# Adding up the routed expert results in memory by the scatter itself, in two buffers used in turn

## The chip, the cores and the metric

The kernel runs on one core of one Trainium2 chip. The metric is the device time of one execution in microseconds, as the median of several runs.

## The reference, cut to what matters

The reference is one transformer layer on 8 sequences of 256 tokens with 256 features (2048 tokens): attention, then a feed-forward part with two shared experts and 16 routed experts, of which each token uses 4. The second part is

```
h = _layernorm(x) * (1 + cb) + sb
scores = sigmoid(h @ gate_w.T)                 # 16 experts in 4 groups, 2 groups kept, 4 experts chosen
w = scores of the 4 chosen / their sum         # cw[t, e]: w at the chosen experts, else 0
hh = silu(einsum('td,edh->teh', h, w1)) * einsum('td,edh->teh', h, w3)
y = einsum('teh,ehd,te->td', hh, w2, cw)       # the sum over each token's 4 routed experts
z = silu(h @ sw1) * (h @ sw3) @ sw2            # the shared experts
out = x + gb * (y + z)
```

The change concerns the sum over a token's four experts in `y`.

## The kernel before

The work is tiled by 128 tokens: 16 tiles (NT). `attention` works through the 8 sequences in a software pipeline. Its routing part runs on VectorE in `choose`, in six groups of tiles: it finds the four experts of each token, writes the weights into `hrow` behind the token's 256 features and, behind those, 16 numbers that say to which row of `y_d` the result of each expert goes: row 4 * token + k for the k-th choice. `send_rows` then scatters each token's row four times from POOL (GpSimd) into `rows_d`, where each expert has its own stretch of rows. At the end of the attention SP (the queue of SyncE) writes zeros over the head of each expert's stretch (L373) and stores the last tiles of x (L362).

`experts` has one unrolled stream of units that TensorE (PE), ScalarE (ACT) and VectorE (DVE) each go through in order: 8 shared tiles, 80 routed tiles (TILES) of 128 rows for one expert each, then the other 8 shared tiles, each shared tile with two units. A unit is: transpose x (L1389), six up matmuls (L1406 to L1408), the gate on ACT and DVE (L1202, L1263 or L1266, and the copy L1268), transpose (L1414, L1415), its split into a high and a low part (L1207, L1272), five down matmuls into `y_ps` (L1429 to L1433). SP loads each routed tile's rows into a ring of six buffers `xin` (L1158). A routed tile's result is copied by ACT to one of three buffers `yout` (L1218), and POOL scatters it to `y_d` by an indirect DMA (L1183), 128 rows of 1 KB. Rows of a tile that hold no token go to spare rows at the end of `y_d`. Only ACT waits on such a scatter, for the buffer: the scatter of tile t - 3 must have landed before tile t is copied.

After the last scatter SP loads, for each of the 16 token tiles in the order of `finals` (0, 8, 1, 9, ...), four rows of 1 KB for each token (`yt`, 512 KB), and the stored x (`x1t`). POOL adds two times two rows (L1187, 128x512) and then two (L1189, 128x256). `combine` on DVE adds the shared result (L1281 from `hrow`, L1285 from `y_ps`), multiplies by `gb` (L1288) and adds x (L1291); SP stores. The pair of tiles (t, t + 8) is combined in DVE's stream four steps behind the unit of tile t + 8, so DVE does it before what follows of the shared units, and the down matmuls of a shared tile wait until the pair two before has left `y_ps`. `gb` comes by eight broadcast loads that SP issues behind the last `xin` (L1161).

Of the kernel before, what the change touches and what calls it, by code (L numbers as in the profile page):

```python
# [53 lines left out]

ROW = HID + 2 * E

# [4 lines left out]
SLOT_ROWS = E * CAP  # L61
Y_ROWS = TOPK * NT * P + TILES * P

# [8 lines left out]
def constants():  # L72

    inv = (1.0 / np.float32(THETA) ** (np.arange(0, D, 2, dtype=np.float32) / np.float32(D))).astype(np.float32)
    freqs = np.arange(S, dtype=np.float32)[:, None] * inv[None, :]
    cos, sin = np.cos(freqs).astype(np.float32), np.sin(freqs).astype(np.float32)
    rope = np.stack([np.concatenate([cos, cos], 1), np.concatenate([-sin, sin], 1)], 1)
    rope = rope.reshape(QT, P, 2, D).transpose(1, 2, 0, 3)
    lower = (np.arange(G)[None, :] < np.arange(G)[:, None]).astype(np.float32)
    key, col = np.arange(P)[:, None], np.arange(SC)[None, :]  # L80
    key, query = np.where(col < K1, key + P, key), np.where(col < K1, col + P, col - K1)
    allowed = (key <= query) & (key > query - WINDOW)
    p = np.arange(P)
    wide = lambda x: np.ascontiguousarray(np.broadcast_to(np.asarray(x, np.float32).reshape(1, -1), (P, np.size(x))))
    fill = P * np.arange(E)
    fill[0] = -1
    return {
        "mask": np.where(allowed, 0.0, -1e5).astype(np.float32),
        "rope": np.ascontiguousarray(rope),
        "ident": np.eye(P, dtype=np.float32),  # L90
        "before": (p[:, None] < p[None, :]).astype(np.float32),
        "small": np.concatenate([
            wide(lower),
            wide(np.arange(E)),
            wide(CAP * np.arange(E) + P),
            wide(fill),
            (TOPK * (np.arange(NT)[None, :] * P + p[:, None])).astype(np.float32),
            (TOPK * NT * P + np.arange(TILES)[None, :] * P + p[:, None]).astype(np.float32),
            p[:, None].astype(np.float32),
            (p[:, None] - P).astype(np.float32),  # L100
            (P * p[:, None]).astype(np.float32),
        ], 1),
    }
# [3 lines left out]
for _name, _n in (("lower", G * G), ("iota", E), ("base", E), ("fill", E), ("tok", NT), ("spare", TILES), ("row", 1), ("behind", 1), ("rows", 1)):  # L107
# [12 lines left out]
ROUTE1 = ("sig biased gmax ggt geq geqm ggt rank gfar*2 maskg masked top*N idx*N idxf onehot picked pick cum*N "  # L120
          "wsel wsum*2 cw id2 id3 ids")
ROUTE2 = "place place_k slot_f slots"
# [11 lines left out]
def build(nc, a, out):  # L134

    with ExitStack() as whole:
# [8 lines left out]
        rows_d = nc.dram_tensor("rows_d", [SLOT_ROWS, ROW], F32, kind="Internal").ap()  # L145
        y_d = nc.dram_tensor("y_d", [Y_ROWS, HID], F32, kind="Internal").ap()

# [23 lines left out]
        })  # L171
        attention(nc, a, mod_rows, x1d, rows_d, hrow, gate_t, ident, w, r)
        sb("w_rest", [P, E - EARLY + SHARED, WE])
# [53 lines left out]

def attention(nc, a, mod_rows, x1d, rows_d, hrow, gate_t, ident, w, r):
    with ExitStack() as ctx:
# [3 lines left out]
        def sem(name):  # L233
# [73 lines left out]
            "c_in w_in wmod_in wo_in ct_tanh_done ct_silu_done cols_mm rows_mm cols_done rows_copied rows_neg_done "  # L307
            "rows_sign_done rows_sign2 rows_done rows_stored x1_stored zeros_set heads_zeroed consts_set pool_consts probs_set wqkvh_done wqkvl_done woh_done wol_done "
            "stats_done mv_done var_eps rstd_done xhat_done xhat_t ht_done hth_done htl_done qkv_mm qkv_done rcos_done rsin_done "
# [17 lines left out]
        def _(sp):  # L327
# [604 lines left out]
def scratch(alloc, n):  # L932

    return named({
        "sig": alloc("sig", [P, n, E], F32), "biased": alloc("biased", [P, n, E], F32), "gmax": alloc("gmax", [P, n, G], F32),
        "g_gt": alloc("g_gt", [P, n, G, G], F32), "g_eq": alloc("g_eq", [P, n, G, G], F32), "rank": alloc("rank", [P, n, G], F32),
        "gfar": alloc("gfar", [P, n, G], F32), "top": alloc("top", [P, n, 8], F32), "idx": alloc("idx", [P, n, 8], U32),
        "idxf": alloc("idxf", [P, n, TOPK], F32), "onehot": alloc("onehot", [P, n, TOPK, E], F32), "picked": alloc("picked", [P, n, E], F32),
        "pick": alloc("pick", [P, n, E], BF16), "wsel": alloc("wsel", [P, n, E], F32), "wsum": alloc("wsum", [P, n], F32),
        "id2": alloc("id2", [P, n, E], F32), "id3": alloc("id3", [P, n, E], F32), "place": alloc("place", [P, n, E], F32),  # L940
        "place_k": alloc("place_k", [P, n, TOPK, E], F32), "slot_f": alloc("slot_f", [P, n, TOPK], F32),
    })
# [7 lines left out]
def choose(dve, r, g, hrow, m):  # L950
# [59 lines left out]
    dve.tensor_tensor(gate_t, g.wsel[:, 0:n], g.wsum[:, 0:n].unsqueeze(2).to_broadcast([P, n, E]), ALU.mult).then_inc(r.worked, 1)  # L1010
    dve.scalar_tensor_tensor(out=g.id2[:, 0:n], in0=g.onehot[:, 0:n, 2], scalar=2.0, in1=g.onehot[:, 0:n, 1], op0=ALU.mult, op1=ALU.add).then_inc(r.worked, 1)
    dve.wait_ge(r.worked, at("id2"))
    dve.scalar_tensor_tensor(out=g.id3[:, 0:n], in0=g.onehot[:, 0:n, 3], scalar=3.0, in1=g.id2[:, 0:n], op0=ALU.mult, op1=ALU.add).then_inc(r.worked, 1)
    dve.wait_ge(r.worked, at("id3"))
    dve.tensor_tensor(hrow[:, here, HID + E:ROW].bitcast(I32), g.id3[:, 0:n], c("tok")[:, here].unsqueeze(2).to_broadcast([P, n, E]), ALU.add).then_inc(r.worked, 1)

# [33 lines left out]
def experts(nc, a, out, mod_rows, x1d, rows_d, y_d, hrow, gate_t, tab, w, r, ident):  # L1050


    with ExitStack() as ctx:
# [19 lines left out]
        def within(name, shape, dt):  # L1073
# [20 lines left out]

        yt = nc.alloc_sbuf_tensor_at("yt", [P, NT, TOPK * HID], F32, offset=address(nc, w.routed))
        x1t = nc.alloc_sbuf_tensor_at("x1t", [P, NT, HID], F32, offset=address(nc, w.routed) + 4 * NT * TOPK * HID)
        gb = w.raw[:].rearrange("p a n -> p (a n)")[:, 0:B * HID].rearrange("p (b h) -> p b h", b=B)
# [9 lines left out]
        s = named({n: sem("f_" + n) for n in (  # L1107
            "xt xh xl up silu hid dup ht hth htl down evac to summed stored added1 added2 gated spread").split()})
        x_in = [sem(f"f_x_in{j}") for j in range(XR)]
        y_sent = [sem(f"f_y_sent{j}") for j in range(YR)]  # L1110
        yt_in = [sem(f"f_yt_in{t}") for t in range(NT)]
# [33 lines left out]
        def _(sp):  # L1145
# [14 lines left out]
            for b in range(B):  # L1160
                sp.dma_start(gb[:, b], mod_rows[b:b + 1, 3].to_broadcast([P, HID])).then_inc(gb_in, 16)  # L1161
            for j in range(YR):
                sp.wait_ge(y_sent[j], 16 * len(range(j, TILES, YR)))
            for c, t in enumerate(finals):
                rows = y_d[t * P * TOPK:(t + 1) * P * TOPK].rearrange("(p k) h -> p (k h)", k=TOPK)
                sp.dma_start(yt[:, t], rows).then_inc(yt_in[t], 16)
                if t % 4 == 0:
                    sp.dma_start(x1t[:, t:t + 4], x1d[t:t + 4].rearrange("t p h -> p t h")).then_inc(x1_in[t // 4], 16)
# [5 lines left out]
        def _(pool):  # L1174
# [5 lines left out]
            for i in range(TILES):  # L1180
                pool.wait_ge(s.evac, FIRST + i + 1)
                pool.wait_ge(s.to, i + 1)
                pool.indirect_dma_start(y_d, bass.IndirectOffsetOnAxis(ap=to[:, i:i + 1], axis=0), yout[:, i % YR], None)\  # L1183
                    .then_inc(y_sent[i % YR], 16)
            for c, t in enumerate(finals):
                pool.wait_ge(yt_in[t], 16)
                pool.tensor_tensor(yt[:, t, 0:2 * HID], yt[:, t, 0:2 * HID], yt[:, t, 2 * HID:4 * HID], ALU.add).then_inc(s.added1, 1)  # L1187
                pool.wait_ge(s.added1, c + 1)
                pool.tensor_tensor(yt[:, t, 0:HID], yt[:, t, 0:HID], yt[:, t, HID:2 * HID], ALU.add).then_inc(s.added2, 1)  # L1189

        @block.scalar
        def _(act):
# [16 lines left out]
            def evacuate(j):  # L1209
# [5 lines left out]
                else:  # L1215
                    if t >= YR:
                        act.wait_ge(y_sent[t % YR], 16 * (t // YR))
                    act.activation(yout[:, t % YR], y_ps[:, j % 2, 0:HID], ACT.Copy).then_inc(s.evac, 1)  # L1218
# [22 lines left out]
        def _(dve):  # L1241
# [257 lines left out]
```

## Time and profile before

| | |
|---|---|
| median of 3 runs | 565.77 us (563.22 to 567.87) |
| profiled execution, its own time | 564.4 us |
| its span | 562.6 us |
| busy: PE, DVE, POOL, ACT | 416.2, 392.8, 296.8, 234.6 us |
| granted clock of TensorE, mean | 0.826 |

The span is what the profile covers; the device time has 1.8 us more. An engine's busy time says little by itself, since the stages have different limits: the rows below are taken stage by stage.

### The profile page before, as it was taken

How to read it: one execution, taken by the hardware profiler on the slowest of the kernel's cores; microseconds unless marked ns; L12 is line 12 of the kernel's file. 1: busy time of each engine (PE TensorE's matmuls, PEld its weight loads, DVE VectorE, ACT ScalarE, POOL GpSimd, SP SyncE). 2: the span in 40 equal slices, each digit the busy share in tenths (PEclk: the TensorE clock that was granted, in tenths of full speed). 3: DMA queues.
4: the chain of work that ended last, by engine and by line, in shares of the span. 5: the costliest groups of instructions: out<-in, count | busy, mean ns of one | idle time of the engine just before them, and what ended most of it. 6: DMA issues, size and time to landing. Idle time of an engine off the chain costs nothing.

```text
span 562.6 us, 10492 instructions
## 1 busy us (share of the span) xinstructions
PE 416.2 (74%) x2841; PEld 380.0 (68%) x2841; DVE 392.8 (70%) x1153; ACT 234.6 (42%) x554; POOL 296.8 (53%) x283
## 2 busy tenths in 40 slices
PE   2537796785689496834273979999999999993664
PEld 2325784765488375723163878999999999993663
DVE  1663787969788685564753767777777777755996
ACT  1334454461445141300323755666666666651211
POOL 1554853715588377353575434444444444446970
PEclk9977777977698575755576998999999999997777
DMA  8404012030322216421145533444444444639911
GB/s 305 125 2 146 5 41 92 1 93 1 112 102 96 89 44 222 170 84 71 59 155 165 166 111 90 141 140 141 141 140 141 141 140 141 163 101 395 374 39 67
DMA packets 38294, 69.68 MB, mean 124 GB/s; under 512 B 5720, under 2 KB 27864, under 8 KB 38112
## 3 DMA queue, kind: packets, MB, share of 16 engines
q1 hardware_dynamic: 31328, 49.08, 27.3%
q0 software_dynamic: 6912, 19.93, 9.6%
q8 instruction: 27, 0.44, 0.4%
q14 instruction: 27, 0.22, 0.1%
HBM read 42.49 MB, written 26.51 MB: 123 GB/s over the span
## 4 chain that ended last, share of the span: by engine, by line
PE 32%; DVE 7%; issue 5%; DMA 3%; POOL 3%; ACT 1%; SPq 0%; DVEq 0%; ACTq 0%
PE up L1406 5%; PE up L1407 5%; PE up L1408 5%; PE xt_ps L1389 3%; PE y_ps L1429 2%; POOL rows_d L1047 2%; PE y_ps L1433 2%; PE y_ps L1432 2%; PE y_ps L1430 2%; PE y_ps L1431 2%; PE ht_ps L1414 2%; PE ht_ps L1415 2%; DMA raw<-in_w_raw 1%; DVE yt L1288 1%; DMA yt<-y_d 1%
## 5 line engine op out<-in xcount | busy, mean ns | idle before, releaser
L1183 POOL DMA_INDIRECT y_d<-yout,to x80 | 77.0, 962 | 85.4 <-ACT yout L1218 85.4
L1047 POOL DMA_INDIRECT rows_d<-hrow,slots x64 | 65.8, 1028 | 35.5 <-issue 16.2
L1197 ACT ACTIVATE f_xh<-xt_ps 128x256 fp32r<-128x256 f32 x96 | 36.8, 384 | 62.0 <-PE xt_ps L1389 61.9
L1202 ACT ACTIVATE silu<-up 128x176 f32<-128x176 f32 x112 | 35.5, 317 | 56.8 <-PE up L1408 56.6
L1406 PE MATMUL up<-w_routed,f_xh 128*128 x160 | 58.4, 365 | 0.0
L1244 DVE TENSOR_TENSOR f_xl<-xt_ps,f_xh 128x256 fp32r<-128x256 f32 x96 | 40.6, 423 | 22.7 <-ACT f_xh L1197 20.3
L405 POOL TENSOR_TENSOR rn<-meansq,minus_half 128x24 f32<-128x24 f32 x8 | 33.4, 4178 | 39.6 <-DVE meansq L611 39.5
L1408 PE MATMUL up<-w_routed,f_xh 128*128 x160 | 52.0, 325 | 0.0
L1407 PE MATMUL up<-w_routed,f_xl 128*128 x160 | 51.9, 325 | 0.0
L207 POOL TENSOR_TENSOR w_routed<-raw,w_routed 128x960 fp32r<-128x960 f32 x16 | 35.9, 2244 | 29.4 <-ACT w_routed L1222 29.0
L1272 DVE TENSOR_TENSOR f_htl<-ht_ps,f_hth 128x256 fp32r<-128x256 f32 x112 | 46.6, 417 | 0.0
L1263 DVE SCALAR_TENSOR_TENSOR hid<-silu,xin,up 128x176 f32<-128x176 f32 x80 | 31.8, 398 | 20.5 <-ACT silu L1202 20.4
L1207 ACT ACTIVATE f_hth<-ht_ps 128x256 fp32r<-128x256 f32 x112 | 43.1, 385 | 1.9 <-PE ht_ps L1415 1.4
L1429 PE MATMUL y_ps<-w_shared,f_hth 112*128 112x256 f32 x32 | 13.2, 412 | 32.9 <-DVE f_htl L1272 32.9
L1268 DVE COPY hid<-hid 128x64 f32<-128x64 f32 x112 | 31.1, 277 | 3.8
L1389 PE MATMUL xt_ps<-ident,xin 128*128 128x128 f32 x160 | 30.7, 273 | 3.5 <-DVE f_xl L1244 3.5
L1218 ACT ACTIVATE yout<-y_ps 128x256 f32<-128x256 f32 x80 | 30.4, 380 | 2.7 <-DMA y_d<-yout,to 2.2
L1414 PE MATMUL ht_ps<-ident,hid 128*128 128x128 f32 x112 | 31.1, 278 | 0.0
L1415 PE MATMUL ht_ps<-ident,hid 128*128 128x128 f32 x112 | 31.1, 277 | 0.0
L1429 PEld LDWEIGHTS y_ps<-w_shared,f_hth 112*128 112x128 f32 x32 | 6.9, 215 | 35.5 <-DVE f_htl L1272 35.5
L1407 PEld LDWEIGHTS up<-w_routed,f_xl 128*128 128x128 f32 x160 | 30.5, 191 | 0.0
L1406 PEld LDWEIGHTS up<-w_routed,f_xh 128*128 128x128 f32 x160 | 30.4, 190 | 0.1
(255 smaller groups left out, 1369.0 us busy)
## 6 DMA issues: line engine op xcount, KB each, us to landing
xin<-rows_d SPq DMA_DIRECT2D x80, 144.0 KB, 2.1
raw<-in_w_raw SPq DMA_DIRECT2D x18, 608.0 KB, 4.2
yt<-y_d SPq DMA_DIRECT2D x16, 512.0 KB, 11.1
mod<-mod_rows SPq DMA_DIRECT2D x8, 384.0 KB, 3.8
rows_d<-zeros SPq DMA_DIRECT2D x16, 144.0 KB, 3.6
x<-in_x SPq DMA_DIRECT2D x4, 512.0 KB, 8.2
x1d<-x SPq DMA_DIRECT2D x8, 256.0 KB, 3.9
x1t<-x1d SPq DMA_DIRECT2D x4, 512.0 KB, 10.5
```

Of the source, the lines that this page charges most:

```text
L1047: pool.indirect_dma_start(rows_d, bass.IndirectOffsetOnAxis(ap=r.slots[:, t, k:k + 1], axis=0), hrow[:, t], None).then_inc(r.sent[t // QT] ...
L1183: pool.indirect_dma_start(y_d, bass.IndirectOffsetOnAxis(ap=to[:, i:i + 1], axis=0), yout[:, i % YR], None)\
L1197: act.activation(xh[:, j % XB], xt_ps[:], ACT.Copy).then_inc(s.xh, 1)
L1207: act.activation(hth[:, u % 2].rearrange("p c q -> p (c q)"), ht_ps[:, u % 2, 0:2 * P], ACT.Copy).then_inc(s.hth, 1)
L1244: dve.tensor_tensor(xl[:, j % XB], xt_ps[:], xh[:, j % XB].bitcast(F32), ALU.subtract).then_inc(s.xl, 1)
L1272: dve.tensor_tensor(htl[:, u % 2].rearrange("p c q -> p (c q)"), ht_ps[:, u % 2, 0:2 * P], hth[:, u % 2].rearrange("p c q -> p (c q)").bit ...
L1389: mm = pe.transpose(xt_ps[:, c], src[:, c * P:(c + 1) * P], ident[:])
L1406: pe.matmul(o, xh[:, j % XB, c], wh, start=(c == 0), stop=False)
L1407: pe.matmul(o, xl[:, j % XB, c], wh, start=False, stop=False)
L1408: mm = pe.matmul(o, xh[:, j % XB, c], wl, start=False, stop=(c == KC - 1))
L1414: pe.transpose(ht_ps[:, u % 2, 0:P], hid[:, u % HB3, 0:P], ident[:])
L1415: pe.transpose(ht_ps[:, u % 2, P:2 * P], hid[:, u % HB3, HA:HW], ident[:]).then_inc(s.ht, 1)
```

## The change

Instead of one `y_d` with four rows for each token there are two buffers of one row for each token, `y_d[0]` and `y_d[1]` (LANES = 2). Both are filled with zeros at the end of the attention, by one DMA each from a 128x256 tile of zeros that is read 17 times. Routed tile i is scattered to buffer i % 2 with the operation add: the DMA reads the row, adds and writes it back. Since two such DMAs must not touch a row at the same time, POOL waits before the scatter of tile i until that of tile i - 2 has landed. The spare rows are now 128 for each buffer. At the end two rows for each token are loaded (in two DMAs of 128 KB), and POOL adds once. The target of a result is the token itself, so one number stands in a row of `hrow` where 16 stood: rows shrink from 288 to 273 numbers, and three operations of `choose` become one copy.

```diff
-ROW = HID + 2 * E
+ROW = HID + E + 1
...
-Y_ROWS = TOPK * NT * P + TILES * P
+
+LANES = 2
+Y_ROWS = NT * P + P
...
-            (TOPK * (np.arange(NT)[None, :] * P + p[:, None])).astype(np.float32),
-            (TOPK * NT * P + np.arange(TILES)[None, :] * P + p[:, None]).astype(np.float32),
+            (np.arange(NT)[None, :] * P + p[:, None]).astype(np.float32),
+            np.broadcast_to(NT * P + p[:, None], (P, TILES)).astype(np.float32),
...
+            for y in y_d:
+                sp.dma_start(y.rearrange("(t p) h -> p t h", p=P), zeros[:, 0:HID].unsqueeze(1).to_broadcast([P, NT + 1, HID])).then_inc(s.y_zeroed, 16)
             store_x1(B - 2)
             store_x1(B - 1)
             sp.wait_ge(s.x1_stored, 16 * B)
             sp.wait_ge(s.heads_zeroed, 16 * E)
+            sp.wait_ge(s.y_zeroed, 16 * LANES)
...
-    dve.scalar_tensor_tensor(out=g.id2[:, 0:n], in0=g.onehot[:, 0:n, 2], scalar=2.0, in1=g.onehot[:, 0:n, 1], op0=ALU.mult, op1=ALU.add).then_inc(r.worked, 1)
-    dve.wait_ge(r.worked, at("id2"))
-    dve.scalar_tensor_tensor(out=g.id3[:, 0:n], in0=g.onehot[:, 0:n, 3], scalar=3.0, in1=g.id2[:, 0:n], op0=ALU.mult, op1=ALU.add).then_inc(r.worked, 1)
-    dve.wait_ge(r.worked, at("id3"))
-    dve.tensor_tensor(hrow[:, here, HID + E:ROW].bitcast(I32), g.id3[:, 0:n], c("tok")[:, here].unsqueeze(2).to_broadcast([P, n, E]), ALU.add).then_inc(r.worked, 1)
+    dve.tensor_copy(hrow[:, here, HID + E:ROW].bitcast(I32), c("tok")[:, here].unsqueeze(2)).then_inc(r.worked, 1)
...
-            for j in range(YR):
-                sp.wait_ge(y_sent[j], 16 * len(range(j, TILES, YR)))
+            for j in range(LANES):
+                sp.wait_ge(y_sent[j], 16 * len(range(j, TILES, LANES)))
             for c, t in enumerate(finals):
-                rows = y_d[t * P * TOPK:(t + 1) * P * TOPK].rearrange("(p k) h -> p (k h)", k=TOPK)
-                sp.dma_start(yt[:, t], rows).then_inc(yt_in[t], 16)
+                for j in range(LANES):
+                    sp.dma_start(yt[:, t, j * HID:(j + 1) * HID], y_d[j][t * P:(t + 1) * P]).then_inc(yt_in[t], 16)
...
-                pool.indirect_dma_start(y_d, bass.IndirectOffsetOnAxis(ap=to[:, i:i + 1], axis=0), yout[:, i % YR], None)\
-                    .then_inc(y_sent[i % YR], 16)
+
+                if i >= LANES:
+                    pool.wait_ge(y_sent[i % LANES], 16 * (i // LANES))
+                pool.indirect_dma_start(y_d[i % LANES], bass.IndirectOffsetOnAxis(ap=to[:, i:i + 1], axis=0), yout[:, i % YR], None,
+                                        compute_op=ALU.add).then_inc(y_sent[i % LANES], 16)
             for c, t in enumerate(finals):
-                pool.wait_ge(yt_in[t], 16)
-                pool.tensor_tensor(yt[:, t, 0:2 * HID], yt[:, t, 0:2 * HID], yt[:, t, 2 * HID:4 * HID], ALU.add).then_inc(s.added1, 1)
-                pool.wait_ge(s.added1, c + 1)
-                pool.tensor_tensor(yt[:, t, 0:HID], yt[:, t, 0:HID], yt[:, t, HID:2 * HID], ALU.add).then_inc(s.added2, 1)
+                pool.wait_ge(yt_in[t], 16 * LANES)
+                pool.tensor_tensor(yt[:, t, 0:HID], yt[:, t, 0:HID], yt[:, t, HID:2 * HID], ALU.add).then_inc(s.added, 1)
...
                     if t >= YR:
-                        act.wait_ge(y_sent[t % YR], 16 * (t // YR))
+                        act.wait_ge(y_sent[(t - YR) % LANES], 16 * ((t - YR) // LANES + 1))
...
-                ids = xin[:, i % XR, bass.ds(e + (HID + E), 1)].bitcast(I32)
+                ids = xin[:, i % XR, HID + E:ROW].bitcast(I32)
```

## Rows read from the trace of the kernel before

**Rows 1.** Stretches: length, busy us (count) per engine, PEclk, DMA share, GB/s

```profile
343.00:491.00 148.00, 148.00 (x1111) 146.45 (x1109) 111.17 (x369) 93.51 (x296) 71.22 (x74) 1.00 0.47 142
...
509.00:518.00 9.00, 0.42 (x4) 0.16 (x2) 5.19 (x9) 0.60 (x2) 5.97 (x6) 0.73 1.03 399
518.00:546.00 28.00, 18.57 (x90) 17.64 (x91) 27.31 (x46) 4.96 (x15) 26.01 (x26) 0.74 0.63 236
546.00:551.00 5.00, 5.00 (x23) 4.91 (x22) 2.67 (x8) 0.70 (x2) 0.00 (x0) 0.53 0.16 56
```

**Rows 2.** Line L1183, scatter of results: ns min/median/max, first and last start

```profile
L1183 POOL DMA_INDIRECT y_d<-yout,to x80: 957/962/987, 343.7 to 501.4; - x80
```

**Rows 3.** Timeline of POOL, amid the routed tiles: start, us, idle before

```profile
401.78 0.96 POOL L1183 DMA_INDIRECT y_d<-yout,to  x1 [1.05 <-ACT yout L1218]
403.80 0.96 POOL L1183 DMA_INDIRECT y_d<-yout,to  x1 [1.05 <-ACT yout L1218]
```

**Rows 4.** DMA view of 500 to 504 us: busy tenths per 0.1 us, queue

```profile
DMA  0000000000000199830000000000099940000000
...
q0 software_dynamic: 96, 0.26, 18.3%
```

**Rows 5.** Chain that ended last, 500 to 563 us: start us, us, what

```profile
501.37 2.41 DMA y_d<-yout,to
...
504.68 7.13 DMA yt<-y_d
```

**Rows 6.** Timeline, 483 to 498 us, queue of SP, POOL and ACT

```profile
483.69 3.83 SPq L1161 DMA_DIRECT2D raw<-mod_rows  x8
...
487.97 0.96 POOL L1183 DMA_INDIRECT y_d<-yout,to  x1 [1.04 <-ACT yout L1218]
...
494.10 0.38 ACT L1218 ACTIVATE yout<-y_ps 128x256 f32<-128x256 f32 x1 [1.26 <-DMA y_d<-yout,to]
```

**Rows 7.** DMA issues of the page: count, KB each, median us to landing

```profile
xin<-rows_d SPq DMA_DIRECT2D x80, 144.0 KB, 2.1
...
rows_d<-zeros SPq DMA_DIRECT2D x16, 144.0 KB, 3.6
```

**Rows 8.** DVE by shape, 514.9 to 542.8 us: busy us, mean ns, idle before

```profile
L1291 DVE TENSOR_TENSOR x1t<-yt,x1t 128x256 f32<-128x256 f32 x7 | 9.7, 1379 | 0.2
L1268 DVE COPY hid<-hid 128x64 f32<-128x64 f32 x6 | 4.3, 721 | 0.2
L1288 DVE TENSOR_TENSOR yt<-yt,raw 128x256 f32<-128x256 f32 x6 | 4.0, 671 | 0.2
L1281 DVE TENSOR_TENSOR yt<-yt,hrow 128x256 f32<-128x256 f32 x3 | 3.7, 1219 | 0.0
```

**Rows 9.** DVE by shape, 552 to 560.5 us, POOL idle

```profile
L1291 DVE TENSOR_TENSOR x1t<-yt,x1t 128x256 f32<-128x256 f32 x6 | 2.5, 425 | 0.2
```

**Rows 10.** DVE copy by shape, 343 to 491 us

```profile
L1268 DVE COPY hid<-hid 128x64 f32<-128x64 f32 x74 | 14.5, 196 | 2.5
```

**Rows 11.** POOL by shape, 504 to 546 us

```profile
L1187 POOL TENSOR_TENSOR yt<-yt 128x512 f32<-128x512 f32 x16 | 21.5, 1346 | 8.1 <-DMA yt<-y_d 8.1
L1189 POOL TENSOR_TENSOR yt<-yt 128x256 f32<-128x256 f32 x16 | 12.3, 771 | 1.3
```

**Rows 12.** Timeline of DVE, last instruction of tile pairs 0, 3 and 7

```profile
514.90 1.37 DVE L1291 TENSOR_TENSOR x1t<-yt,x1t 128x256 f32<-128x256 f32 x1
...
541.03 1.38 DVE L1291 TENSOR_TENSOR x1t<-yt,x1t 128x256 f32<-128x256 f32 x1
...
560.01 0.42 DVE L1291 TENSOR_TENSOR x1t<-yt,x1t 128x256 f32<-128x256 f32 x1
```

**Rows 13.** Timeline of SP's queue, end of the attention

```profile
218.36 10.59 SPq L373 DMA_DIRECT2D rows_d<-zeros  x16
232.20 27.14 SPq L362 DMA_DIRECT2D x1d<-x  x2
```

**Rows 14.** DVE groups by line: busy us, mean ns

```profile
L1013 DVE SCALAR_TENSOR_TENSOR id<-onehot,id 128x32 f32<-128x32 f32 (+1 forms) x5 | 1.0, 205 | 0.2
```

More of the change, by code:

```diff
@@ L120 @@
 ROUTE1 = ("sig biased gmax ggt geq geqm ggt rank gfar*2 maskg masked top*N idx*N idxf onehot picked pick cum*N "
-          "wsel wsum*2 cw id2 id3 ids")
+          "wsel wsum*2 cw ids")
 ROUTE2 = "place place_k slot_f slots"
@@ L145, in build @@
         rows_d = nc.dram_tensor("rows_d", [SLOT_ROWS, ROW], F32, kind="Internal").ap()
-        y_d = nc.dram_tensor("y_d", [Y_ROWS, HID], F32, kind="Internal").ap()
+        y_d = [nc.dram_tensor(f"y_d{j}", [Y_ROWS, HID], F32, kind="Internal").ap() for j in range(LANES)]
         hrow = sb("hrow", [P, NT, ROW])
@@ L171, in build @@
         })
-        attention(nc, a, mod_rows, x1d, rows_d, hrow, gate_t, ident, w, r)
+        attention(nc, a, mod_rows, x1d, rows_d, y_d, hrow, gate_t, ident, w, r)
         sb("w_rest", [P, E - EARLY + SHARED, WE])
@@ L225, in after, with attention @@
         eng.wait_ge(sem, count)
-def attention(nc, a, mod_rows, x1d, rows_d, hrow, gate_t, ident, w, r):
+def attention(nc, a, mod_rows, x1d, rows_d, y_d, hrow, gate_t, ident, w, r):
     with ExitStack() as ctx:
@@ L307, in attention @@
             "c_in w_in wmod_in wo_in ct_tanh_done ct_silu_done cols_mm rows_mm cols_done rows_copied rows_neg_done "
-            "rows_sign_done rows_sign2 rows_done rows_stored x1_stored zeros_set heads_zeroed consts_set pool_consts probs_set wqkvh_done wqkvl_done woh_done wol_done "
+            "rows_sign_done rows_sign2 rows_done rows_stored x1_stored zeros_set heads_zeroed y_zeroed consts_set pool_consts probs_set wqkvh_done wqkvl_done woh_done wol_done "
             "stats_done mv_done var_eps rstd_done xhat_done xhat_t ht_done hth_done htl_done qkv_mm qkv_done rcos_done rsin_done "
@@ L939, in scratch @@
         "pick": alloc("pick", [P, n, E], BF16), "wsel": alloc("wsel", [P, n, E], F32), "wsum": alloc("wsum", [P, n], F32),
-        "id2": alloc("id2", [P, n, E], F32), "id3": alloc("id3", [P, n, E], F32), "place": alloc("place", [P, n, E], F32),
+        "place": alloc("place", [P, n, E], F32),
         "place_k": alloc("place_k", [P, n, TOPK, E], F32), "slot_f": alloc("slot_f", [P, n, TOPK], F32),
@@ L1092, in experts @@
         first_row = within("first_row", [P, TILES], F32)
-        yt = nc.alloc_sbuf_tensor_at("yt", [P, NT, TOPK * HID], F32, offset=address(nc, w.routed))
-        x1t = nc.alloc_sbuf_tensor_at("x1t", [P, NT, HID], F32, offset=address(nc, w.routed) + 4 * NT * TOPK * HID)
+        yt = nc.alloc_sbuf_tensor_at("yt", [P, NT, LANES * HID], F32, offset=address(nc, w.routed))
+        x1t = nc.alloc_sbuf_tensor_at("x1t", [P, NT, HID], F32, offset=address(nc, w.routed) + 4 * NT * LANES * HID)
         gb = w.raw[:].rearrange("p a n -> p (a n)")[:, 0:B * HID].rearrange("p (b h) -> p b h", b=B)
@@ L1107, in experts @@
         s = named({n: sem("f_" + n) for n in (
-            "xt xh xl up silu hid dup ht hth htl down evac to summed stored added1 added2 gated spread").split()})
+            "xt xh xl up silu hid dup ht hth htl down evac to summed stored added gated spread").split()})
         x_in = [sem(f"f_x_in{j}") for j in range(XR)]
-        y_sent = [sem(f"f_y_sent{j}") for j in range(YR)]
+        y_sent = [sem(f"f_y_sent{j}") for j in range(LANES)]
         yt_in = [sem(f"f_yt_in{t}") for t in range(NT)]
@@ L1276, in combine @@
                 t = finals[c]
-                dve.wait_ge(s.added2, c + 1)
+                dve.wait_ge(s.added, c + 1)
                 total = yt[:, t, 0:HID]
```

## The prediction

> **What bounds the kernel now.** I read the table of stretches first, since the change touches two stages with different limits. From 343 to 491 us, the routed tiles, PE is busy all of the time at full clock: 1111 matmuls in 148.0 us, 0.133 us each, 15 for a tile, so 2.0 us for a tile [rows 1]. Nothing that POOL or the DMAs do there costs anything as long as it fits into 2.0 us for each tile. POOL's scatter takes 0.96 us of them [rows 2], and POOL starts one every 2.02 us after sitting idle for 1.05 us until ACT has copied the tile [rows 3]. From 509 to 546 us it is the other way round: from 509 to 518 PE does 4 matmuls, and the DMAs are full; from 518 to 546 DVE is busy 27.3 of 28 us and POOL 26.0, PE 18.6 [rows 1]. There the chain runs over the landing of the last scatter and of the second load of `yt` [rows 5], then over DVE's combining.
>
> DVE is full there because of POOL. The same kinds of operations take 1379 ns (L1291), 1219 (L1281), 671 (L1288) and 721 (the copy L1268) while POOL adds [rows 8]; L1291 takes 425 ns when POOL is idle [rows 9], and the copy 196 in the routed stage [rows 10]. I take 0.42 us for the other two as well, being of the shape of L1291. Each pair of tiles has two of L1291, two of L1288, one of L1281 and two of the copy: 2 x 0.954 + 2 x 0.246 + 0.80 + 2 x 0.525 = 4.25 us of stretching. From the last operation of pair 0 to that of pair 3 pass 541.03 - 514.90 = 26.13 us, 8.71 for a pair [rows 12]; without the stretching that would be 4.46.
>
> **The steady stage.** The new wait puts POOL's scatter of tile i behind the landing of that of tile i - 2. Scatters start 2.0 us apart, so the wait costs nothing while a scatter lands within 4.0 us of its start (call this time L). Behind the waiting POOL stand only later scatters; ACT waits for them at tile t - 3, and PE for ACT through `y_ps`. Once L is over 4.0, this backs up within some tiles, and every tile takes L/2: the cost is 78 x (L/2 - 2.0). For the plain scatter L is 2.41 [rows 5]. Its parts can be seen in the DMA view, where little else runs: the data of the scatter started at 501.37 move from 502.9 to 503.3, so 1.5 us pass before, 0.4 in it, and 0.5 after [rows 4, 5]. An added scatter isn't in the trace. Below, L is 2.41 if the read of the row is hidden; above, if a full load of rows comes first, 2.1 + 2.41 = 4.5 [rows 5, 7]. I take 3.3: the data stretch twice (+0.4), and half a microsecond for the reading to come back, since it is the same descriptors on the same queue, and the load's 2.1 has its own issue and landing in it. So +0 here. The instruction itself (0.96) may take longer for three descriptors than for two; it has 1.05 us to spare.
>
> The page "Collectives: The Full Stack" of the Trainium skill, section "The bandwidth ceiling: the fold count and why AG ≠ RS ≠ AR", says that an add in the DMA engine costs no cycles of its own but needs two source reads, so that it runs at half the rate of a copy. By that rule L would be 2.41 + 0.4 = 2.8 and this stage again free; no row of this trace has an adding DMA.
>
> **Where L is long already.** Beside the eight broadcast loads issued from 483.69 on, the scatter started at 487.97 holds up ACT until 494.10: L is up to 6.1 us [rows 6]. With three buffers that costs little; with two lanes, three tiles queue behind one another. I put the scatters of before in a list and moved each behind the landing two before; with L of 3.3 afterwards they catch up at 1.65 us each and the last starts some 1.1 us later. Bounds 0 to 3. With the longer landing of the last one (+0.9), the loads of `yt` start **2.0 us later**.
>
> **Pair 0.** Its two tiles now need 4 x 128 KB and 512 KB of x instead of 2 x 512 and 512, with another 512 KB of x interleaved in both. That is 0.5 to 0.75 MB less; at 399 GB/s [rows 1] -1.9 us of the 7.13 [rows 5]. POOL's 1346 ns operation is gone [rows 11]: -1.35. DVE's last operation isn't stretched: -0.95. Two more DMAs to issue: +0.45. Sum -3.75, with the +2.0 **-1.8 us**: pair 0 ends at 514.5 instead of 516.3.
>
> **Pairs 1 to 7.** They took 560.43 - 516.27 = 44.2 us [rows 12]. POOL's work falls from 21.5 + 12.3 to 12.3 us [rows 11], paced by the loads (14 x 256 KB and 1 MB of x at 399 GB/s, 12 us), so it ends near 526. Until then DVE is still stretched, but behind operations of 0.77 us and not 1.35: 2.5 us a pair rather than 4.25. Pair 1 takes 7.0, pair 2 5.7 (half of it beside POOL). Pairs 3 to 5 could run at DVE's 4.46. What is late next is PE: a shared tile has 28 matmuls, 3.7 us at 2.4 GHz but 6.1 at 1.2 GHz (5.00 us for 23, granted clock 0.53 [rows 1]). The clock fell in the idle stretch from 509 to 518 (0.73 [rows 1]); with shorter waits it should be up most of the time. I take 5.0 each, bounds 4.46 and 6.1. Pairs 6 and 7 only drain, with six operations of 0.42 each: 2.9 a pair. Together 7.0 + 5.7 + 15.0 + 5.8 = 33.5: **-10.7 us**.
>
> **What costs nothing.** The two zero DMAs move 4.46 MB behind the heads' zeros, which SP has issued by 229; at 399 GB/s they take 11 us, at the pace of the heads (2.3 MB in 10.6 us [rows 13]) 20, so they land by 249. What hides them is the attention of the last sequence: SP doesn't get to issue the last store of x before 259 [rows 13], and the block can't end before it. The store in front of that stands behind them and has as much time. Uncovered they would cost up to 20 us; bounds 0 to +2. Between the heads' zeros and these, POOL's scatters of rows share the DMAs, but nobody waits for those before the end of the stage. In `choose` three operations of about 0.2 us [rows 14] go in each of six groups and one comes: some 2.5 us less on DVE, between -2.5 and 0 on the path; I take 0, since the last group's work lies beside POOL's queue of 16 row scatters. Rows of 1092 bytes instead of 1152: 5% fewer bytes, perhaps worse aligned; the load's 2.1 us stands against six buffers of 2.0 us each [rows 7].
>
> **Sum.** -1.8 - 10.7 = -12.5. Profiled execution 564.4, after 551.9; it lies 1.4 us under the median, so from the median 565.8 - 12.5 = **553.3 us**. Its own range: -2.5 (choose), -2.5 (little stretching), -1.6 (clock up at once) below, and +3.5 (stretching as before), +3.3 (PE at 1.2 GHz), +2 (the broadcasts, zeros) above, not all at once: 545 to 561.
>
> **The rivals.**
> 1. *The lane's wait takes the place of the loads.* L is over 4.0, so that each routed tile takes L/2. For it: PE has no slack in this stage, L was 6.1 beside the broadcasts [rows 1, 6], and the upper bound is 4.5. Against: 1.6 us of margin over 2.41. It eats up the gain at L = 4.0 + 2 x 12.5 / 78 = 4.32; at L = 5 it costs 39 us: 592. Chance 0.24, of it 0.07 between 4.0 and 4.32 (553 to 566) and 0.17 above.
> The page "DMA: Bandwidth & Descriptors" of the Trainium skill, section "Latency and other measured facts", has reads of HBM return after 0.2 us on average and 2 us at high load. By the first figure L is 3.0, by the second 4.8, which would be an estimate of 31 us more, 584; that L depends on the load agrees with the 6.1 us of rows 6.
> 2. *POOL becomes the bound by its own instruction*: an added scatter takes it over 2.0 us to issue instead of 0.96. At 2.5 us 78 x 0.5 = 39 us more: 592. Nothing in the trace speaks for a doubling; chance 0.06.
> 3. *The combining isn't shortened*: DVE keeps its 8.7 us a pair because small POOL operations stop it as often, or PE at 1.2 GHz paces it at 6 to 7 us. Then only -1.8 and a few us remain: 561 to 564. The rows of DVE speak against it, since the long ones follow the long POOL operations. Chance 0.09.
>
> Forecast 0.61. A measurement of this kernel tells about 1%, 5.7 us, from no change: faster below 560.1, slower above 571.4. Faster: 0.61 + 0.04 + 0.01 = 0.66. Slower: 0.15 of rival 1, 0.06 of rival 2, 0.21. Within: 0.13. The range: 0.03 lies below 545; up to 576 (L = 4.6) it leaves out another 0.17.
>
> **What the profile after would show.** L1183: starts 2.0 us apart from 343 to 491, with idle time ended by ACT; if instead a DMA ends it, rival 1; a mean well over 0.96, rival 2. The first load of `yt` at about 505.8; POOL with 16 operations of 0.77, done near 526; DVE's L1291 near 0.43 from pair 3 on; pairs 3 to 5 at 4.5 to 6 us; last L1291 near 548. TensorE's clock from 515 on decides whether it is 4.5 or 6. Wrong would make it a scatter that lands late beside other traffic, or zeros that still run at 260.

## The result and the profile after

The changed kernel takes 595.11 us (median of 4 runs, 589.82 to 598.5) beside 566.82 us before (565.77 us is the median of three of its four runs): 1.050 times as long, 95% interval 1.039 to 1.061. The profiled execution takes 592.05 us, its span 590.3 us, against 562.6.

Three stretches account for the 27.7 us between the spans. The first scatter of a result starts at 347.2 us instead of 343.7 (+3.5); from the first to the last one pass 194.2 us instead of 157.7 (+36.5); from the last to the end of the span 48.9 instead of 61.2 (-12.3). Of the 36.5 us, 29.4 lie between the second scatter and the 71st (167.7 us instead of 138.3), where in the kernel before every tile takes 2.0 us, and 7.1 in the last nine intervals, beside and behind the eight broadcast loads (24.6 instead of 17.4).

**The routed stage.** The page's costliest groups, with idle time before them and its main releaser, for the scatter and for ACT's copy in front of it:

```profile
L1187 POOL DMA_INDIRECT y_d<-yout,to x80 | 124.0, 1550 | 75.1 <-ACT yout L1220 66.1
...
L1220 ACT ACTIVATE yout<-y_ps 128x256 f32<-128x256 f32 x80 | 30.8, 385 | 88.9 <-DMA y_d<-yout,to 77.7
```

The scatter takes POOL 1550 ns, where it took 962 [rows 2], and ACT, which had waited 2.2 us in all for a landing, now waits 77.7. The same two waits in the view of waits from 347 to 541 us (total, times, longest):

```profile
ACT yout L1220 <- DMA y_d<-yout,to: 77.7, 62, 4.4
POOL y_d L1187 <- ACT yout L1220: 66.1, 68, 4.0
```

POOL's timeline (start, duration, idle before) has the places from which the pitch can be read:

```profile
366.65 1.55 POOL L1187 DMA_INDIRECT y_d<-yout,to  x1 [1.68 <-ACT yout L1220]
...
422.08 1.55 POOL L1187 DMA_INDIRECT y_d<-yout,to  x1 [0.58 <-ACT yout L1220]
```

```profile
516.88 1.55 POOL L1187 DMA_INDIRECT y_d<-yout,to  x1 [1.30 <-ACT yout L1220]
522.41 1.55 POOL L1187 DMA_INDIRECT y_d<-yout,to  x1 [3.98 <-ACT yout L1220]
525.88 1.55 POOL L1187 DMA_INDIRECT y_d<-yout,to  x1 [1.93 <-ACT yout L1220]
...
541.44 1.55 POOL L1187 DMA_INDIRECT y_d<-yout,to  x1 [0.30 <-issue]
```

From the ninth scatter (366.65) to the 71st (516.88) pass 150.2 us, 2.42 for a tile instead of 2.0 [rows 3]. The idle time is put down to ACT's copy, and that is to be read with care: the copy that ends just before 422.08 is that of the tile after the one being scattered. It and the scatter are let go by the same thing, the landing of the tile two before the scattered one (lanes1 below tells the two apart). The chain that ended last shows it, where the profile passes through ACT:

```profile
453.43 3.88 DMA y_d<-yout,to
...
457.39 0.39 ACT yout L1220
457.79 0.28 issue
```

The scatter started at 453.43 lands after 3.88 us, and the next in the chain starts 0.76 us later (458.07). Nor is the cycle always that short: it is 2 x 2.42 = 4.84 us on average. The trace of this run lacks the landings of many scatters; that of after_gb below, with the same two buffers, has all 80: 3.7 us at the least, 3.9 in the median, 5.0 at the most, 4.05 on average, and 0.81 on average from there to the next start. That makes 4.86. How the landing is made up stands in the DMA view of 541 to 546 us (busy tenths per 0.125 us), where no row loads run:

```profile
DMA  0000079894899640040079995899941000000000
DMA packets 289, 0.28 MB, mean 56 GB/s; under 512 B 32, under 2 KB 288, under 8 KB 288
...
q0 software_dynamic: 288, 0.26, 47.4%
```

The scatter started at 541.44 moves its data from 543.5 to 544.85: 2.05 us until it begins (before: 1.5), 1.35 in it (0.4), and the rest to the landing 0.4 (0.5) [rows 4]. The bytes counted are those of before, 0.26 MB for two scatters [rows 4], but they go in other packets (the 289th is of another queue). Before, the same view of two scatters had

```profile
DMA packets 96, 0.26 MB, mean 66 GB/s; under 512 B 32, under 2 KB 32, under 8 KB 96
```

In the packet records that is 32 packets of 4 KB and 16 of 4 bytes for a plain scatter, and 128 of 1 KB, a row each, and 16 of 4 bytes for an adding one. Each of the 16 DMA engines has eight data packets of 0.145 us on average, one after another, instead of two of 0.18: 1.2 us instead of 0.4. How much of the 0.145 us is the read of the old row can't be told, since no run scatters plainly in packets of 1 KB. The page's queue row shows it for the whole kernel:

```profile
q0 software_dynamic: 14592, 19.44, 17.2%
```

The row scatters have 64 x 48 = 3072 of these packets as before; the remaining 11520 are 144 for each of 80 results, three times the 48 of before. In the busy stretches (length; busy us and count of PE, PEld, DVE, ACT, POOL; PEclk; DMA share; GB/s) PE has 4.5 us without work in 50 in the routed stage, and its busy time, which is modelled, is stretched as well: 314 matmuls in 45.5 us are 0.145 each, against 0.133 [rows 1]:

```profile
400.00:450.00 50.00, 45.50 (x314) 41.91 (x313) 27.77 (x105) 24.80 (x86) 32.55 (x21) 1.00 0.64 116
554.00:568.00 14.00, 10.01 (x56) 9.41 (x56) 13.35 (x29) 3.28 (x10) 10.56 (x14) 0.77 1.01 329
```

The second stretch lies behind the end of pair 0: there the DMAs are full and DVE is busy for 13.35 of 14 us.

**The end.** POOL has only the short addition left; the long operations of DVE are short again after that, and pair 0 and the last pair end with these:

```profile
L1191 POOL TENSOR_TENSOR yt<-yt 128x256 f32<-128x256 f32 x16 | 12.7, 811 | 13.0 <-DMA yt<-y_d 12.9
```

```profile
L1293 DVE TENSOR_TENSOR x1t<-yt,x1t 128x256 f32<-128x256 f32 x16 | 8.4, 528 | 2.0 <-DMA x1t<-x1d 1.6
```

```profile
554.24 0.43 DVE L1293 TENSOR_TENSOR x1t<-yt,x1t 128x256 f32<-128x256 f32 x1 [0.96 <-DMA x1t<-x1d]
...
587.68 0.42 DVE L1293 TENSOR_TENSOR x1t<-yt,x1t 128x256 f32<-128x256 f32 x1
```

L1293 took 1379 ns beside POOL before, and takes 528 on average now [rows 8]. From the end of pair 0 (554.67) to that of pair 7 (588.10) pass 33.4 us, against 44.2 [rows 12]. Pair 0 ends with x, whose load is in the chain there:

```profile
547.65 6.49 DMA x1t<-x1d
```

**The zeros.** SP's queue shows the two zero DMAs behind the heads' zeros, and the stores of x behind them:

```profile
222.54 11.03 SPq L375 DMA_DIRECT2D rows_d<-zeros  x16
233.61 8.41 SPq L377 DMA_DIRECT2D y_d<-zeros  x2
242.06 22.61 SPq L364 DMA_DIRECT2D x1d<-x  x2
```

The heads' zeros start 4.2 us later than before (218.36 [rows 13]), so this execution was late before the zeros of the change were issued.

### The profile page after: what moved, and what is told of

The parts are those of the page before. It is cut to its first block, busy times and chain, and to the rows that moved or that the text cites. A ratio compares the mean times of both kernels' runs of the same rounds, so it can differ in the third digit from the quotient of the medians.

```text
span 590.3 us, 10402 instructions
## 1 busy us (share of the span) xinstructions
PE 438.8 (74%) x2841; PEld 390.2 (66%) x2841; DVE 369.5 (63%) x1141; ACT 228.9 (39%) x554; POOL 324.0 (55%) x267
## 4 chain that ended last, share of the span: by engine, by line
PE 26%; DMA 11%; issue 6%; DVE 5%; ACT 2%; another core or an unknown queue 1%; SPq 0%; POOL 0%; DVEq 0%; ACTq 0%
DMA y_d<-yout,to 10%; PE up L1408 4%; PE up L1410 4%; PE up L1409 4%; PE y_ps L1431 3%; PE xt_ps L1391 3%; PE y_ps L1435 2%; PE y_ps L1434 2%; PE y_ps L1432 2%; PE y_ps L1433 2%; PE ht_ps L1417 1%; PE ht_ps L1416 1%; DMA x1t<-x1d 1%; DVE hid L1270 1%
## 5 line engine op out<-in xcount | busy, mean ns | idle before, releaser
L1187 POOL DMA_INDIRECT y_d<-yout,to x80 | 124.0, 1550 | 75.1 <-ACT yout L1220 66.1
L1220 ACT ACTIVATE yout<-y_ps 128x256 f32<-128x256 f32 x80 | 30.8, 385 | 88.9 <-DMA y_d<-yout,to 77.7
L1408 PE MATMUL up<-w_routed,f_xh 128*128 x160 | 59.5, 372 | 0.0
L410 POOL TENSOR_TENSOR rn<-meansq,minus_half 128x24 f32<-128x24 f32 x8 | 33.4, 4178 | 41.0 <-DVE meansq L616 41.0
L1410 PE MATMUL up<-w_routed,f_xh 128*128 x160 | 52.7, 329 | 0.0
L1431 PE MATMUL y_ps<-w_routed,f_hth 112*128 x80 | 30.7, 383 | 18.4 <-issue 9.7
L1431 PEld LDWEIGHTS y_ps<-w_routed,f_hth 112*128 112x128 f32 x80 | 15.3, 191 | 28.8 <-issue 27.8
L1431 PE MATMUL y_ps<-w_shared,f_hth 112*128 112x256 f32 x32 | 12.7, 395 | 26.9 <-DVE f_htl L1274 26.5
```

The lines of the kernel that those rows point to most:

```text
L1187: pool.indirect_dma_start(y_d[i % LANES], bass.IndirectOffsetOnAxis(ap=to[:, i:i + 1], axis=0), yout[:, i % YR], None, compute_op=ALU.add) ...
L1408: pe.matmul(o, xh[:, j % XB, c], wh, start=(c == 0), stop=False)
L1410: mm = pe.matmul(o, xh[:, j % XB, c], wl, start=False, stop=(c == KC - 1))
L1431: pe.matmul(o, hth[0:HA, q, 0], at(HA, O2A, O2B), start=begin, stop=False)
```

## The experiments

Where "routed stretch" is said, it is from the start of the first to that of the last scatter of a result, "the end" from there to the end of the span. The shares of before are taken against executions of the kernel before in the same session (medians of 564.28 and 565.34 us). Each run has one profiled execution.

**plain_two: only the add taken away.**

```diff
-                pool.indirect_dma_start(y_d[i % LANES], ..., yout[:, i % YR], None,
-                                        compute_op=ALU.add).then_inc(y_sent[i % LANES], 16)
+                pool.indirect_dma_start(y_d[i % LANES], ..., yout[:, i % YR], None).then_inc(y_sent[i % LANES], 16)
```

> The changed kernel, but the scatter only writes and doesn't add (so the last of a token's results in each buffer stands for the sum: that part of the computation is left out). Both buffers, the wait for the scatter two before, the smaller loads at the end are kept. My theory now: the wait costs because an adding scatter lands 3.9 to 4.5 us after its start and POOL needs 0.7 us from landing to the next start, 4.66 us for two tiles; a plain one lands after 2.4 and with 0.7 stays under 4.0. Then tiles come every 2.0 us, and the time is that of before less what the end saves: 552 to 560 us. Rival: any wait between scatters costs, whatever the landing takes: 585 or more.

Measured: 556.33 us, 0.986 of before (0.979 to 0.994). The line of the scatter (ns min/median/max, first and last start), and who let POOL go:

```profile
L1187 POOL DMA_INDIRECT y_d<-yout,to x80: 956/958/983, 342.1 to 502.9; - x80
...
  ACT yout L1219: 84.0, 75
```

The routed stretch is 160.8 us and the end 48.7. With the wait in place but a plain scatter behind it, the loss of the steady stage is gone: from the second scatter to the 71st pass 138.4 us, as before (138.3). The wait costs nothing where the landing is short. It isn't free beside the broadcasts, where plain scatters too land late: the last nine intervals take 20.4 us instead of 17.4, which is nearly all of the 3.1 us by which the routed stretch is longer than before. The first scatter starts at 342.1, the earliest of all kernels here, with the zeros and the shorter rows of the change in it, and after_gb, which is the changed kernel up to there, has it at 344.4. So the 3.5 us before the first scatter don't come from the change; in the ten profiled executions of this study it starts between 342.1 and 347.2.

**lanes3: three buffers.**

```diff
-LANES = 2
+LANES = 3
...
-                pool.tensor_tensor(yt[:, t, 0:HID], yt[:, t, 0:HID], yt[:, t, HID:2 * HID], ALU.add).then_inc(s.added, 1)
+                for j in range(1, LANES):
+                    if j > 1:
+                        pool.wait_ge(s.added, c * (LANES - 1) + j - 1)
+                    pool.tensor_tensor(yt[:, t, 0:HID], yt[:, t, 0:HID], yt[:, t, j * HID:(j + 1) * HID], ALU.add).then_inc(s.added, 1)
...
-                dve.wait_ge(s.added, c + 1)
+                dve.wait_ge(s.added, (c + 1) * (LANES - 1))
```

> The changed kernel with three buffers in turn, so that a scatter waits for that three before; POOL adds three rows at the end in two operations, three loads of 128 KB a tile. Theory (the wait's cycle): three tiles share 4.66 us, under 6.0, so that PE's 2.0 us bounds again: 595 less 34, plus 3 at the end: 562 to 568 us. Rival (the load of adding scatters on DMAs and POOL: 1.3 us of all DMA engines and 1.55 us of POOL for each tile): the pitch stays at 2.2 to 2.35 us and the time at 580 to 597.

Measured: 563.18 us, 0.998 of before (0.994 to 1.001). The scatter's line, and the first part of the routed stretch, where PE is busy throughout with 1034 matmuls in 139.5 us, 0.135 each, and the DMAs to 86%:

```profile
L1187 POOL DMA_INDIRECT y_d<-yout,to x80: 1545/1549/1629, 344.5 to 509.0; - x80
```

```profile
344.50:484.00 139.50, 139.50 (x1034) 137.85 (x1034) 99.09 (x344) 86.86 (x275) 106.53 (x69) 0.99 0.86 134
```

So the adding scatters fit under PE's 2.0 us once three of them share a cycle; the rival, that their load alone sets the pitch, falls. The routed stretch is 164.5 us, 6.8 more than before. Of these 1.7 lie between the first scatter and the second (3.7 us apart), before any landing is waited for, and 4.7 in the last nine intervals, beside the eight broadcasts (POOL's timeline):

```profile
488.85 1.54 POOL L1187 DMA_INDIRECT y_d<-yout,to  x1 [0.44 <-DVE to L1256]
490.85 1.55 POOL L1187 DMA_INDIRECT y_d<-yout,to  x1 [0.46 <-ACT yout L1223]
495.75 1.55 POOL L1187 DMA_INDIRECT y_d<-yout,to  x1 [3.36 <-ACT yout L1223]
499.64 1.55 POOL L1187 DMA_INDIRECT y_d<-yout,to  x1 [2.34 <-ACT yout L1223]
```

The scatter of 499.64 uses the buffer of that of 488.85, which by ACT's copy at 498.96 landed 10.0 us after its start.

**lanes1: one buffer.**

```diff
-LANES = 2
+LANES = 1
...
-            for c, t in enumerate(finals):
-                pool.wait_ge(yt_in[t], 16 * LANES)
-                pool.tensor_tensor(yt[:, t, 0:HID], yt[:, t, 0:HID], yt[:, t, HID:2 * HID], ALU.add).then_inc(s.added, 1)
...
-                dve.wait_ge(s.added, c + 1)
+                dve.wait_ge(yt_in[t], 16)
```

> The changed kernel with one buffer: every scatter waits for the one before; one row for each token at the end, and POOL adds nothing there. Theory (the wait's cycle): a tile takes the whole cycle of 4.66 us, 78 x 2.33 = 182 us more than the changed kernel, 765 to 785 us in all. Rival (load of DMAs and POOL): the pitch stays at 2.35 and the time near 590.

Measured: 779.09 us, 1.377 of before. Here the profile gives the landing itself, and the chain consists of almost nothing else:

```profile
L1187 POOL DMA_INDIRECT y_d<-yout,to x80: 1545/1549/1630, 345.2 to 736.8; - x80
...
DMA to landing us min/median/max: 3.7/3.9/8.2
```

```profile
478.64 3.89 DMA y_d<-yout,to
...
482.62 0.39 ACT yout L1217
483.01 0.28 issue
483.29 3.87 DMA y_d<-yout,to
```

Scatters start 4.65 us apart here, 3.89 to land and 0.76 from landing to start (391.6 us for 79, 4.96 on average, since some land late). POOL needs the landing of the scatter before and the copy of its own tile, which was made two tiles earlier; ACT's copy in the chain is that of the tile two ahead. That this copy isn't what lets POOL go shows where ACT is late:

```profile
384.48 3.91 DMA y_d<-yout,to
...
388.75 0.39 ACT yout L1217
389.15 0.00 issue
```

The scatter lands at 388.39, the copy starts 0.36 us later and ends just before 389.15, and POOL's next scatter starts at 389.15 all the same, 0.76 us behind the landing. So it is in 75 of the 79 cases, whether the copy ends 0.29 or 0.01 us before. What POOL does in the 0.76 us is not to be seen in the profile.

**add_alone: only the add, without any wait.** The kernel before, results in rows of their own.

```diff
+            NZ = TOPK * NT
+            sp.dma_start(y_d[0:NZ * P].rearrange("(t p) h -> p t h", p=P), zeros[:, 0:HID].unsqueeze(1).to_broadcast([P, NZ, HID])).then_inc(s.y_zeroed, 16)
...
-                pool.indirect_dma_start(y_d, ..., yout[:, i % YR], None)\
+                pool.indirect_dma_start(y_d, ..., yout[:, i % YR], None, compute_op=ALU.add)\
```

> The kernel before with only the operation add in its scatter: every result still goes to a row of its own, four a token, so there is no wait between scatters; the 8192 rows are filled with zeros by one DMA of 8.4 MB behind the heads' zeros (the spare rows aren't). Theory (the wait's cycle): POOL's instruction 1.55 us and the landing near 4 are there, but the pitch is 2.0 and ACT waits for no buffer (needs a landing under 5.3); the end is as before: 566 to 575 us, the few us for more traffic. Rival (the load): pitch 2.2 to 2.35, 585 or more.

Measured: 571.52 us, 1.012 of before (1.009 to 1.016). The scatter's line with what waited for it, and the stretch up to the broadcasts:

```profile
L1186 POOL DMA_INDIRECT y_d<-yout,to x80: 1545/1549/1630, 344.3 to 506.2; - x80
...
  ACT yout L1221: 5.5, 3
```

```profile
344.30:484.00 139.70, 139.70 (x1049) 138.25 (x1048) 104.79 (x349) 88.68 (x280) 108.33 (x70) 1.00 0.90 140
```

POOL's 1.55 us and a DMA share of 0.90 are there, and PE is busy in all of 139.7 us. So neither POOL's instruction nor the traffic stretches the steady stage. The routed stretch is 161.9 us; the 4.2 us more than before all lie in the last nine intervals (21.6 us instead of 17.4), where ACT, which has three buffers `yout`, waits 2.51 and 2.57 us for landings beside the broadcasts.

**after_gb, lanes3_gb, before_gb: the broadcasts spread.** The same edit in the changed kernel, in the one with three buffers and in the one before:

```diff
-            sp.wait_ge(w.low_b, NE)
-            for b in range(B):
-                sp.dma_start(gb[:, b], mod_rows[b:b + 1, 3].to_broadcast([P, HID])).then_inc(gb_in, 16)
+                if i >= 20 and (i - 20) % 5 == 0 and (i - 20) // 5 < B:
+                    b = (i - 20) // 5
+                    if b == 0:
+                        sp.wait_ge(w.low_b, NE)
+                        sp.wait_ge(w.low, NE)
+                    sp.dma_start(gb[:, b], mod_rows[b:b + 1, 3].to_broadcast([P, HID])).then_inc(gb_in, 16)
```

> The changed kernel with the eight broadcast loads of gb issued between the loads of tiles 20, 25, ... 55 instead of all together behind the last one. Theory: the lane's cycle of 4.66 us holds at every tile, and the broadcasts add only the one long landing of 8.2 us near the end: 4 to 7 us less, 588 to 591 us, pitch 2.33 as before. Rival: the broadcasts are most of the loss: under 575 us.

> Three buffers in turn, and the broadcasts spread as in after_gb. Theory: with three buffers the pitch is 2.0 but for the 6 us that are lost beside the broadcasts (scatters at 490.85, 495.75, 499.64 us in the run with three buffers); without them 563.2 - 6 = 557 us, range 554 to 559. Rival: the adding scatters lose the same time beside single broadcasts spread over the stage: 562 to 565.

> The kernel before with the broadcasts spread in the same way. Theory: it loses about 3 us there now (a wait of 0.55, 1.26 and 0.38 us in ACT, pitch 2.66 and 2.13 once each) and makes some of it good after: 1 to 3 us less, 561.5 to 564. Rival: nothing, 564 to 566.

Measured: after_gb 589.07 us, 1.044 of before (1.037 to 1.051); lanes3_gb **554.31 us, 0.981** (0.975 to 0.986); before_gb 563.73, 0.997 (0.994 to 1.000). Their scatter lines in this order:

```profile
L1190 POOL DMA_INDIRECT y_d<-yout,to x80: 1546/1550/1630, 344.4 to 537.2; - x80
```

```profile
L1190 POOL DMA_INDIRECT y_d<-yout,to x80: 1545/1549/1629, 344.1 to 503.7; - x80
```

```profile
L1186 POOL DMA_INDIRECT y_d<-yout,to x80: 958/958/983, 344.9 to 502.3; - x80
```

In after_gb the routed stretch is 192.8 us, 1.4 less than in the changed kernel, and the intervals of the two ratios overlap: the broadcasts are not the main loss there. Its landings are the ones used above:

```profile
DMA to landing us min/median/max: 3.7/3.9/5.0
```

The last nine intervals are 4.6 us shorter (19.9 instead of 24.6), but the tiles between the second scatter and the 71st, beside which the single broadcasts now run, take 1.5 us more (2.45 us for a tile, where I had expected 2.33), and the second scatter comes 1.7 us later behind the first. I had expected 4 to 7 us less; how much spreading them is worth with two buffers one profiled execution each doesn't settle. With three buffers the stretch falls from 164.5 to 159.6 us, as expected; the time fell by more (8.9 us between medians that were taken on different chips); the profiled execution, at 557.7, is the second longest of six. In before_gb the gain is at the edge of what can be told. In lanes3_gb the last scatters show the next limit:

```profile
499.93 1.55 POOL L1190 DMA_INDIRECT y_d<-yout,to  x1 [0.30 <-DMA y_d<-yout,to]
501.85 1.55 POOL L1190 DMA_INDIRECT y_d<-yout,to  x1 [0.38 <-DMA y_d<-yout,to]
```

They start 1.85 to 1.93 us apart, and 1.85 is what POOL needs at the least, 1.55 for the instruction and 0.30 between two of them, with any number of buffers: adding scatters have little to spare under 2.0 us.

**one_add: the end by itself.** The kernel before, without the long addition.

```diff
-                pool.tensor_tensor(yt[:, t, 0:2 * HID], yt[:, t, 0:2 * HID], yt[:, t, 2 * HID:4 * HID], ALU.add).then_inc(s.added1, 1)
-                pool.wait_ge(s.added1, c + 1)
```

It leaves out two of each token's four routed results.

> The kernel before without POOL's 128x512 addition at the end (so only two of a token's four routed results are added: the other two are left out); all 512 KB a tile are still loaded. Theory: what shortened the end by 12.3 us in the changed kernel is POOL's shorter work, which lets go of DVE; the pairs take about 6.4 and then 5 us as there: 553 to 557 us. Rival: it was the halved load (8.4 to 4.2 MB) that shortened it: 560 to 564, pairs still at 8 us or more.

Measured: 551.60 us, 0.975 of before (0.969 to 0.981). The scatter's line; the load of `yt` (KB each, us to landing); DVE's last operation, and the last ones of pair 0 and pair 7:

```profile
L1183 POOL DMA_INDIRECT y_d<-yout,to x80: 962/962/987, 345.5 to 503.7; - x80
```

```profile
yt<-y_d SPq DMA_DIRECT2D x16, 512.0 KB, 11.0
```

```profile
L1289 DVE TENSOR_TENSOR x1t<-yt,x1t 128x256 f32<-128x256 f32 x16 | 8.2, 511 | 0.6
```

```profile
515.42 0.42 DVE L1289 TENSOR_TENSOR x1t<-yt,x1t 128x256 f32<-128x256 f32 x1
...
548.37 0.42 DVE L1289 TENSOR_TENSOR x1t<-yt,x1t 128x256 f32<-128x256 f32 x1
```

The time is 1.4 us below the range that I had given. With all 8.4 MB loaded and an unchanged landing of 11 us, the end is 47.2 us, shorter still than in the changed kernel. It was POOL's long operation that held DVE, not the loads. The other half, the loads halved and the long addition kept, was not run.

**All runs, stage by stage.** From the starts of the 80 scatters of results (us):

| run | second to 71st | last nine intervals |
|---|---|---|
| before | 138.3 | 17.4 |
| after | 167.7 | 24.6 |
| plain_two | 138.4 | 20.4 |
| lanes3 | 138.7 | 22.1 |
| lanes1 | 345.6 | 41.4 |
| add_alone | 138.3 | 21.6 |
| after_gb | 169.2 | 19.9 |
| lanes3_gb | 138.5 | 17.5 |
| before_gb | 138.3 | 17.1 |
| one_add | 138.3 | 17.4 |

Only where adding scatters wait for the landing one or two before does the steady stage take longer.

## Why the prediction was wrong

The forecast of 553.3 us failed, and 595.1 lies above the range; rival 1 happened. That its price for L = 5, 592 us, comes near is luck in part: L is 4.05 us on average in after_gb, and it is the whole cycle, which the rival didn't have, that is 4.86.

**The step that failed is the one in "The steady stage"**: "the wait costs nothing while a scatter lands within 4.0 us of its start", with L taken as 3.3. Two terms in it were off: L was too small, and the time from a landing to the next start was put at nothing.
- L itself is 3.8 to 3.9 us and often more. I had put +0.4 on the data stretch and +0.5 on the read. The trace has +0.95 on the stretch (0.4 to 1.35), +0.55 before it, along with a POOL instruction that is 0.59 longer, and nothing after. That is inside the bounds of 2.41 to 4.5, but I took the value on no row. "The same descriptors" was wrong: 32 data packets became 128. The Trainium skill has for the reduce step of a ReduceScatter ("Collectives: The Full Stack", section "The bandwidth ceiling: the fold count and why AG ≠ RS ≠ AR") that the add needs two source reads and so runs at half the rate of a copy. By that rule the stretch would be 0.8 us, an estimate; the measured one is 1.35, and the measurement decides.
- The limit is not 4.0 but 3.24: POOL starts 0.76 us after a landing, which I had left out altogether. A wait that has just been met isn't a start. Even the L of 3.3 that I took lies above that limit. With L + 0.76 = 4.65 against 4.0 the sum of that paragraph gives 78 x 0.33 = 25 us, and with the average cycle of 4.84 78 x 0.42 = 33; plain_two (2.4 + 0.8 = 3.2 against 4.0), lanes3 (4.65 against 6.0) and lanes1 (4.65 against 2.0) fall on the side that this sum gives them.

**Where L is long already**: the mechanism was right and the size too small. The scatters started at 514.04 and 516.88, beside the broadcasts, each hold up the next in their buffer, those of 522.41 and 525.88. The first lands after 7.6 us by ACT's copy at 521.74, the second after 8.24 by the chain:

```profile
516.88 8.24 DMA y_d<-yout,to
```

The starts are 5.5 and 3.5 us apart instead of 2.42, about 4 us; I had 1.1, with bounds 0 to 3. In plain_two, where no steady loss mixes in, it is 3.0. My list let the scatters catch up at L/2 = 1.65 us each, without the 0.76.

**Pair 0**: the -1.8 us had 1.1 in it for a later last scatter; from the last scatter's start on it was -2.9. Measured from there, the end of pair 0 comes after 13.2 us instead of 14.9, -1.7. The landing took 1.4 us more and not 0.9. And the -1.9 for fewer bytes, the upper end of my 0.5 to 0.75 MB, is hardly there: one_add has 12.2 us with all bytes loaded, -2.7 by POOL's and DVE's parts alone (I had -2.3). In the changed kernel the rows of the second tile do land earlier (6.3 us behind the first load's issue, 7.5 in one_add), but then DVE waits 0.96 us for x, whose load takes 6.49 us.

**Pairs 1 to 7**: forecast 33.5 us, measured 33.4, and by parts too: pairs 1 and 2 take 12.8 us (12.7 forecast), 3 to 5 15.0 (15.0), 6 and 7 5.7 (5.8). Within these the pairs differ (6.3 and 6.5 for 7.0 and 5.7). TensorE's clock, which I wanted up most of the time, was granted at 0.55 in pair 1, at 1.00 in pair 2 and at 0.81 and 0.87 in pairs 3 and 4, which take 5.1 and 5.8 us. POOL letting go of DVE is shown by one_add. From the last scatter on the forecast was -2.9 - 10.7 = -13.6, and 12.3 us were given back, only that the routed stage took 36.5.

**What costs nothing**: right for the zeros and for `choose`, as far as 3 us can be told: SP issued the zeros in 8.4 us, and the first scatter of plain_two, with the same parts, is early. The gain that three fewer operations of `choose` might bring isn't to be seen either.

**Rival 2** (POOL bound by its instruction) didn't happen, as add_alone shows, but was nearer than I thought: the instruction grew by 60%, to 1.55 us, which with 0.30 between two is 1.85 of 2.0. **Rival 3** fell: the pairs 1 to 3 take 6.3, 6.5 and 5.1 us and not 8.7.

**The range** reached lower than its own terms: those below the forecast add up to 6.6 us, 546.7, where I wrote 545.

## What to carry to other kernels

Before a wait is put between steps that overlapped, write down the whole cycle that it closes (start to landing, landing to next start) and divide by the number of buffers: two buffers had a cycle of 4.65 to 4.86 us for a limit of 4.0, three for 6.0. The third turned 5% slower into no change, and with the broadcasts spread into 1.9% faster. A step that isn't in the trace should be tried by itself, or be taken at the worse of its bounds, when the stage behind it has no slack. And look at what an engine off the path does to its neighbour: the gain at the end came from the long operation that POOL no longer does beside DVE, and not from the halved loads.

## What the runs showed of the hardware

- An indirect scatter of 128 rows of 1 KB with the operation add takes POOL 1.55 us against 0.96, has 128 data packets of 1 KB against 32 of 4 KB, keeps the DMAs busy for 1.35 us against 0.4, and lands 3.9 us after its start in the median (3.7 to 5.0 in after_gb) against 2.4.
- Two such scatters start at least 1.85 us apart, 0.30 from the end of one to the start of the next; plain ones 1.26.
- From the landing that POOL waits for to its next scatter 0.76 us pass (75 of 79 cases with one buffer), while ACT starts 0.08 us after the same landing (landed at 457.31, copy at 457.39).
- Eight broadcast loads of 128 KB, each from one row, hold up scatters that are under way, plain ones as well: to 6.0 us after their start in the kernel before and 7.6 in plain_two, 8.2 with adding scatters and one or two buffers, and 10.0 with three, where more of them are under way.
